# Group 3's high and low parts by converting and adding transfers, with the order of work laid out anew

## The chip, the core and the metric

The kernel runs on one core of a Trainium2 chip. The metric is the time of the whole program on the device in microseconds, the median of several executions. The engines are TensorE (PE, matrix products and transposes), VectorE (DVE), ScalarE (ACT) and GpSimd (POOL); SyncE (SP) only issues transfers. Each engine works off its own instructions in order and waits on semaphores for the others.

## The reference

Four steps on `x` of shape (4, 512, 256, 4) and a text `txt` of shape (4, 77, 256), all float32.

```python
h = einsum('bhid,oi,od->bho', x, weighted_sum, weight)      # tokens
h = concatenate([h, txt], axis=1)                            # 4 x 589 x 256
# attention-like block on n = layernorm(h)
hid  = relu(n @ gate_w1 + b1); gate = sigmoid(hid @ gate_w2 + b2)
glob = gate * (n @ U_w) * cumsum(n @ V_w, axis=1)
h = h + conv3(n, conv_w) + glob @ out_w + out_b
# quantised product on m = layernorm(h): int8 with a scale for each row of m
# and each column of rhs, exact integer product, then scaled back
h = h + int8_product(m, rhs)
```

## The kernel before

The 4 x 512 token rows are cut into eight **groups** of 256 (two to a batch, g0 to g7). A group's token product contracts over 1024 values: eight blocks of 128 (`kc` 0 to 7), each of which multiplies 2 x 128 rows by a 128 x 256 weight. Group 0 uses plain float32 products (L907). Groups 1 to 7 use three cheaper products for each block: `x_high` by `w_high` (L923), `x_high` by `w_low` (L925) and `x_low` by `w_high` (L927), where `x_high` is `x` rounded to a shorter format and `x_low` the rest. One block is called a **step** here: 64 steps in all, six products each from group 1 on. Blocks 0 to 3 of a group are its first half, 4 to 7 its second half; the halves are loaded and waited for apart.

There are two ways to the two parts. For groups 1 to 3, SyncE loads `x` into `x_sb` (L352), ScalarE rounds it into `x_high` (`chip_high`, L527), and VectorE (`chip_low`, L735) or, for group 3, GpSimd (`pool_low`, L435) subtracts. For groups 4 to 7 no engine sees `x`: GpSimd issues a transfer that converts `x` into `x_high` (`load_high`, L430), ScalarE writes minus `x_high` into `x_low` (`negate`, L538), and GpSimd issues a second transfer that adds `x` onto it (`add_x`, L441). Both parts lie in rings of three slots. The constant `BY_DMA` is the first group that goes the second way.

After its token product each group goes through statistics (VectorE, L709 and L712), one over the root of the variance and a shift (GpSimd, L404, L405, L463), normalising (ScalarE, L634), transposing (TensorE, L973), moving (ScalarE, L595), the hidden product (TensorE, L989), relu, running sums (VectorE, L784, L835), and for each batch the gate product (TensorE, L997), the sigmoid (ScalarE, L609) and the product of gate and sums (`gated`, GpSimd, L415, L421), which ScalarE and VectorE split in a high part (L618) and a low part (L818). Each batch then has three **items** (two of 256 rows, one of 77 text rows; 0 to 11): convolution (`local`, L1014) and output product (`mix`, L1027) on TensorE, a second layer norm, the row's maximum and step (VectorE, L824, L826, L828), rounding (GpSimd, L482), a transpose (L1041), conversion to integers (ScalarE, L627), the integer product (L1057), its scaling (VectorE, L861) and the last addition (`fin`, GpSimd, L495), then the store. For the last four items VectorE does the last addition itself (L851).

What is done in which order is written out by hand in the tables `GROUP_AT`, `ITEM_AT`, `TXT_AT`, `RHS_AT` and `WARM_AT`: a number for each stage and group or item, its **place**. Each engine runs through the places in rising order. On TensorE a step begins every 16 places, so that place 241 lies after step 15. On the others places are numbered more loosely. An instruction that has to wait holds up all behind it on its engine.

Of the kernel before, what the change touches and what calls it, by code (L numbers as in the profile page):

```python
# [10 lines left out]
ALU = mybir.AluOpType  # L11
# [23 lines left out]
    move=(7, 16, 27, 39, 51, 63, 75, 82),  # L35
    hidden=(321, 403, 497, 626, 754, 849, 1012, 1021),
    relu=(11, 20, 32, 42, 62, 66, 80, 84),
    sums=(11, 17, 27, 33, 46, 49, 62, 66),
    gates=(-1, 417, -1, 657, -1, 898, -1, 1023),
    sigmoid=(-1, 22, -1, 45, -1, 68, -1, 86),  # L40
    gated=(-1, 9, -1, 24, -1, 38, -1, 53),
    high=(24, 25, 49, 50, 69, 71, 89, 90),
    low=(19, 20, 37, 38, 54, 58, 69, 72),
    mid=(8, 18, 37, 40, 52, 67, 77, 83),
    tap0=(9, 15, 28, 31, 44, 50),
    tap2=(10, 16, 34, 36, 48, 51),
# [12 lines left out]
    put=(-1, -1, 33, -1, -1, 57, -1, -1, 79, -1, -1, 95),  # L59
    conv=(418, 467, 545, 722, 724, 817, 961, 1013, 1018, 1024, 1028, 1038),  # L60
    mix=(466, 468, 546, 723, 725, 818, 962, 1017, 1020, 1026, 1033, 1039),
    stats=(21, 22, 26, 39, 40, 47, 57, 64, 65, 71, 76, 79),
    rstd=(12, 16, 21, 30, 31, 40, 44, 50, 58, 59, 66, 67),
    centre=(28, 30, 36, 53, 55, 64, 73, 85, 87, 92, 98, 101),
    keep=(29, 31, 38, 54, 56, 65, 74, 93, 96, 97, 100, 104),
    scale=(24, 25, 29, 43, 45, 55, 61, 67, 70, 74, 78, 81),
    round=(15, 19, 22, 34, 37, 46, 47, 54, 57, 62, 65, 69),
    lscale=(17, 27, 28, 42, 43, 51, 52, 55, 60, 63, 68, 70),
    turn=(625, 659, 755, 897, 1011, 1015, 1019, 1027, 1031, 1037, 1042, 1045),
    ints=(43, 47, 58, 70, 76, 81, 88, 91, 94, 99, 102, 103),  # L70
    product=(658, 753, 820, 1010, 1014, 1022, 1025, 1029, 1035, 1040, 1043, 1046),
    out=(35, 42, 56, 60, 63, 68, 73, 75, 77, 80, 82, 83),
# [18 lines left out]
def early_fusion_kernel(nc, x0, x, ws, wt, txt, par, rhs, out, B, HI, T, D, ND, GH, R):  # L91
# [45 lines left out]
    with ExitStack() as ctx:  # L137
# [251 lines left out]
        def _(pool):  # L389
# [54 lines left out]
            for place in range(PLACES):  # L444
                for g in groups(place, "cast"):
                    load_high(g)
                for g in groups(place, "pool_low0"):
                    pool_low(g, 0)
                for g in groups(place, "pool_low1"):
                    pool_low(g, 1)  # L450
# [705 lines left out]
```

## Time and profile before

| | |
|---|---|
| median of 3 executions | 107.63 us (106.84 to 108.24) |
| profiled execution | 108.13 us, of which the span of the trace is 106.3 us |
| TensorE busy, of the span | 93.8 us, 88% |
| VectorE | 87.9 us, 83% |
| ScalarE | 76.2 us, 72% |
| GpSimd | 68.4 us, 64% |
| mean granted TensorE clock | 0.979 of 2.4 GHz |
| moved by the 16 DMA engines | 16.30 MB |

The busy time is what an engine's instructions took; what is not busy was waiting. Loads of weights on TensorE overlap its products. Time before the first and after the last traced instruction makes up the difference between 108.13 and 106.3.

### The profile page before, as it was taken

The numbers are of one execution on the slowest core, as the hardware profiler recorded it, in microseconds if no ns is written. First come the engines' busy times: TensorE is split into PE (matmuls) and PEld (weight loads), VectorE is DVE, ScalarE is ACT, GpSimd is POOL, SyncE is SP. The second block draws the span as 40 slices with busy tenths as digits, with TensorE's granted clock in tenths as the row PEclk, the third lists the DMA queues.
The fourth block names the chain that finished last, engine by engine and source line by source line (L and its number), as shares of the span: only waits on it lengthen the run. The fifth ranks groups of instructions, "written<-read, shape, count | busy, mean of one in ns | idle before, by whom it ended". The sixth has DMA issues, their size and how long they took to land.

```text
span 106.3 us, 2136 instructions
## 1 busy us (share of the span) xinstructions
PE 93.8 (88%) x686; PEld 85.4 (80%) x686; DVE 87.9 (83%) x224; ACT 76.2 (72%) x150; POOL 68.4 (64%) x131
## 2 busy tenths in 40 slices
PE   5999999998999999899945999699998889959780
PEld 5988899996969989899925999599896768849660
DVE  2456996969999887699999499999999999997731
ACT  1319739998979998899892969182898998656420
POOL 2000049099798469998993749903799979985840
PEclk9999999999999999999998599999999999999998
DMA  2999998038099499969959913894000050112223
GB/s 69 314 288 374 251 372 331 29 100 297 12 173 294 133 190 180 328 133 213 310 59 196 206 59 31 172 215 82 0 21 8 3 197 0 39 42 99 87 98 128
DMA packets 7849, 16.30 MB, mean 153 GB/s; under 512 B 823, under 2 KB 4767, under 8 KB 7839
## 3 DMA queue, kind: packets, MB, share of 16 engines
q0 software_dynamic: 2304, 8.39, 35.3%
q1 hardware_dynamic: 5103, 7.52, 21.3%
q10 hardware_dynamic: 432, 0.27, 0.9%
q8 instruction: 5, 0.08, 0.3%
q14 instruction: 5, 0.04, 0.1%
HBM read 13.76 MB, written 2.41 MB: 152 GB/s over the span
## 4 chain that ended last, share of the span: by engine, by line
PE 36%; DVE 20%; DMA 15%; POOL 10%; ACT 8%; issue 7%; SPq 0%; DVEq 0%; POOLq 0%
DMA x_sb<-x_dram 7%; DMA x_low<-x_dram 7%; PE h_ps L907 7%; DVE glob L818 4%; DVE convT L796 4%; PE acc_ps L1062 3%; DVE stats L709 3%; ACT xn L634 3%; POOL rstd L405 3%; PE h_ps L923 3%; POOL x_high L430 2%; PE h_ps L925 2%; PE h_ps L927 2%; DVE tmp L861 2%; PE uvg_ps L989 2%
## 5 line engine op out<-in xcount | busy, mean ns | idle before, releaser
L923 PE MATMUL h_ps<-w_high,x_high 128*128 128x256 f32 x112 | 33.7, 301 | 0.2 <-DMA x_low<-x_dram 0.2
L925 PE MATMUL h_ps<-w_low,x_high 128*128 128x256 f32 x112 | 31.8, 284 | 0.0
L927 PE MATMUL h_ps<-w_high,x_low 128*128 128x256 f32 x112 | 31.7, 283 | 0.0
L923 PEld LDWEIGHTS h_ps<-w_high,x_high 128*128 128x128 f32 x112 | 21.6, 193 | 1.0 <-issue 0.3
L925 PEld LDWEIGHTS h_ps<-w_low,x_high 128*128 128x128 f32 x112 | 21.7, 193 | 0.2
L927 PEld LDWEIGHTS h_ps<-w_high,x_low 128*128 128x128 f32 x112 | 21.6, 193 | 0.0
L405 POOL TENSOR_TENSOR rstd<-rstd,exponent 128x2 f32<-128x2 f32 (+2 forms) x21 | 16.3, 774 | 1.7
L404 POOL TENSOR_SCALAR rstd<-mv 128x2 f32<-128x2 f32 (+2 forms) x21 | 5.2, 249 | 17.9 <-DVE mv L712 17.0
L709 DVE BATCH_NORM_STATS2 stats<-h_ps 128x6 f32<-128x256 f32 (+1 forms) x36 | 13.7, 417 | 3.0 <-PE h_ps L927 2.1
L644 ACT ACTIVATE xc<-h_ps,mv 128x256 f32<-128x256 f32 (+1 forms) x20 | 8.6, 471 | 7.2 <-DVE mv L712 7.2
L796 DVE SCALAR_TENSOR_TENSOR convT<-xnT,par_sb,convT 128x255 f32<-128x255 f32 (+1 forms) x24 | 12.0, 548 | 0.8 <-ACT convT L588 0.7
L482 POOL TENSOR_SCALAR v<-xc,qmul 128x256 f32<-128x256 f32 (+1 forms) x20 | 10.9, 596 | 2.1 <-DVE qmul L828 1.8
L495 POOL TENSOR_TENSOR fin<-tmp,x_sb 128x512 f32<-128x512 f32 (+1 forms) x8 | 9.9, 1248 | 0.0
L634 ACT ACTIVATE xn<-h_ps,shift,rstd 128x256 f32<-128x256 f32 x16 | 8.1, 557 | 2.4 <-POOL shift L463 2.3
L441 POOL DMA_DIRECT2D x_low<-x_dram x8 | 7.6, 989 | 2.9 <-ACT x_low L538 2.7
L989 PE MATMUL uvg_ps<-xnT,par_sb 128*128 128x256 f32 x32 | 8.6, 391 | 1.0 <-issue 1.0
L588 ACT ACTIVATE convT<-xnT,par_sb 128x255 f32<-128x255 f32 (+1 forms) x16 | 9.3, 630 | 0.2
L538 ACT ACTIVATE x_low<-x_high 128x1024 fp32r<-128x1024 f32 x8 | 8.5, 1056 | 0.0
L618 ACT ACTIVATE glob<-glob 32x256 fp32r<-32x256 f32 (+1 forms) x16 | 7.2, 448 | 1.5 <-POOL glob L415 1.0
L1027 PE MATMUL h_ps<-outw,glob 96*128 96x256 f32 (+1 forms) x20 | 5.5, 344 | 2.7 <-DVE glob L818 2.7
L1014 PE MATMUL h_ps<-ident,convT 128*128 128x128 f32 (+1 forms) x40 | 7.9, 287 | 0.0
L907 PE MATMUL h_ps<-w_tok,x_sb 128*128 128x256 f32 x32 | 7.8, 405 | 0.0
(110 smaller groups left out, 217.2 us busy)
## 6 DMA issues: line engine op xcount, KB each, us to landing
x_high<-x_dram POOLq DMA_DIRECT2D x8, 512.0 KB, 5.2
x_low<-x_dram POOLq DMA_DIRECT2D x8, 512.0 KB, 5.6
x_sb<-x_dram SPq DMA_DIRECT2D x6, 512.0 KB, 7.5
out_dram<-fin SPq DMA_DIRECT2D x8, 256.0 KB
x_sb<-x_dram SPq DMA_DIRECT2D x3, 256.0 KB, 3.9
par_sb<-par_dram SPq DMA_DIRECT2D x1, 325.0 KB, 8.2
txt_sb<-txt_dram SPq DMA_DIRECT2D x1, 308.0 KB
out_dram<-fin SPq DMA_DIRECT2D x4, 77.0 KB
```

The lines of the kernel that those rows point to most:

```text
L405: nc.gpsimd.tensor_tensor(out_ap, out_ap, exponent[0:out_ap.shape[0], 0:out_ap.shape[1]], ALU.pow).then_inc(done, 1)
L482: last = nc.gpsimd.tensor_scalar(v[0:rows, j % 2, t, :], xc[0:rows, j % 4, t, :], qmul[0:rows, j, t:t + 1], ROUND + LOW_ZERO, ALU.mult, AL ...
L495: nc.gpsimd.tensor_tensor(fin[0:rows, j % 4, 0:nt, :], tmp[0:rows, j % 2, 0:nt, :], h2[0:rows, j % 4, 0:nt, :], ALU.add).then_inc(fin_pool, 1)
L588: nc.scalar.activation(convT[:, b % 2, c, lo:hi], xnT[:, c, b, 1 + lo:1 + hi], ACT.Identity, scale=conv[:, c, 1:2], bias=outb[:, c:c + 1]) ...
L634: last = nc.scalar.activation(xn[:, g % 2, t, :], h_of(g)[:, t, :], ACT.Identity, scale=rstd1[:, 2 * g + t:2 * g + t + 1], bias=shift1[:, ...
L709: last = nc.vector.bn_stats(stats[0:rows, t, :], src(t))
L796: nc.vector.scalar_tensor_tensor(out=convT[:, b % 2, c, lo:hi], in0=xnT[:, c, b, lo + tap:hi + tap], scalar=conv[:, c, tap:tap + 1], in1=c ...
L907: last = nc.tensor.matmul(h_of(g)[:, t, :], x_sb[:, g % X_SLOTS, kc, t * P:(t + 1) * P], w_tok[:, kc, :], start=(kc == 0 and t == 0), stop ...
L923: nc.tensor.matmul(h_of(g)[:, t, :], x_high[:, g % RING, kc, at], w_high[:, kc, :], start=(kc == 0 and t == 0), stop=False, skip_group_che ...
L925: nc.tensor.matmul(h_of(g)[:, t, :], x_high[:, g % RING, kc, at], w_low[:, kc, :], start=False, stop=False, skip_group_check=True)
L927: last = nc.tensor.matmul(h_of(g)[:, t, :], x_low[:, g % RING, kc, at], w_high[:, kc, :], start=False, stop=(kc == KC - 1), skip_group_che ...
L989: last = nc.tensor.matmul(uvg_ps[:, 0:PAIR], wcat[:, c, :], xnT[:, c, b, 1 + half * PAIR:1 + (half + 1) * PAIR], start=(c == 0), stop=(c = ...
```

## The change

Group 3 goes the second way: `BY_DMA` falls from 4 to 3. SyncE's two loads of group 3, ScalarE's two roundings and GpSimd's two subtractions go; two converting transfers, two negations on ScalarE and two adding transfers come. The function `pool_low` goes. All tables of places are new numbers, with the same stages in them.

```diff
 GROUP_AT = dict(
-    pool_low0=(-1, -1, -1, 4),
-    pool_low1=(-1, -1, -1, 6),
-    stats=(3, 6, 14, 23, 32, 41, 52, 59),
-    rstd=(0, 3, 8, 14, 23, 32, 39, 45),
-    norm=(5, 12, 23, 35, 48, 60, 72, 78),
-    turn=(241, 353, 465, 577, 721, 819, 1009, 1016),
+    stats=(2, 7, 14, 25, 32, 43, 53, 60),
+    rstd=(0, 4, 9, 16, 23, 32, 40, 47),
+    norm=(4, 13, 23, 36, 45, 60, 71, 79),
+    turn=(193, 322, 433, 593, 674, 817, 1009, 1017),
...
-    chip_high0=(-1, 1, 4, 10),
-    chip_high1=(-1, 2, 6, 15),
+    chip_high0=(-1, 1, 5),
+    chip_high1=(-1, 2, 7),
     chip_low0=(-1, 1, 5),
-    chip_low1=(-1, 2, 8),
-    cast=(-1, -1, -1, -1, 2, 7, 13, 20),
-    negate0=(-1, -1, -1, -1, 14, 26, 41, 59),
-    add0=(-1, -1, -1, -1, 5, 11, 25, 33),
-    negate1=(-1, -1, -1, -1, 21, 34, 44, 61),
-    add1=(-1, -1, -1, -1, 10, 18, 26, 36),
+    chip_low1=(-1, 3, 8),
+    cast=(-1, -1, -1, 1, 3, 8, 15, 22),
+    negate0=(-1, -1, -1, 10, 17, 29, 43, 59),
+    add0=(-1, -1, -1, 5, 7, 14, 27, 33),
+    negate1=(-1, -1, -1, 14, 22, 35, 49, 61),
+    add1=(-1, -1, -1, 6, 11, 17, 28, 35),
 )
...
-    fin=(29, 35, 41, 48, 49, 56, 61, 64),
+    fin=(30, 34, 41, 49, 51, 52, 63, 64),
...
-BY_DMA = 4
+BY_DMA = 3
...
             sp.dma_start(rhs_sb[:, :, :], rhs).then_inc(rhs_loaded, 16)
-            sp.wait_ge(tok_done, 1)
-            for n in range(2):
-                load_x(sp, 3, n)
...
-            def pool_low(g, n):
-                pool.wait_ge(chip_high_ready[n], g - PLAIN + 1)
-                nc.gpsimd.tensor_tensor(x_low[:, g % RING, HALF_KC[n], :], x_sb[:, g % X_SLOTS, HALF_KC[n], :],
-                                        x_high[:, g % RING, HALF_KC[n], :].bitcast(F32),
-                                        ALU.subtract).then_inc(chip_low_ready[g - PLAIN][n], 1)
```

**GpSimd's queue at the start**, from the root of group 0's variance on. L430 is the converting transfer, L441 the adding one, L435 the subtraction; before:

```order
L463 TENSOR_SCALAR shift<-mv,rstd 128x1 x2
L404 TENSOR_SCALAR rstd<-mv 77x4
L405 TENSOR_TENSOR rstd<-rstd,exponent 77x4
L430 DMA x_high<-x_dram 128x1024 x2
L404 TENSOR_SCALAR rstd<-mv 128x2
L405 TENSOR_TENSOR rstd<-rstd,exponent 128x2
L463 TENSOR_SCALAR shift<-mv,rstd 128x1 x2
L435 TENSOR_TENSOR x_low<-x_sb,x_high 128x1024
L441 DMA x_low<-x_dram 128x1024
L435 TENSOR_TENSOR x_low<-x_sb,x_high 128x1024
L430 DMA x_high<-x_dram 128x1024 x2
```

Now (L425 is the converting transfer, L430 the adding one):

```order
L448 TENSOR_SCALAR shift<-mv,rstd 128x1 x2
L425 DMA x_high<-x_dram 128x1024 x2
L399 TENSOR_SCALAR rstd<-mv 77x4
L400 TENSOR_TENSOR rstd<-rstd,exponent 77x4
L425 DMA x_high<-x_dram 128x1024 x2
L399 TENSOR_SCALAR rstd<-mv 128x2
L400 TENSOR_TENSOR rstd<-rstd,exponent 128x2
L448 TENSOR_SCALAR shift<-mv,rstd 128x1 x2
L430 DMA x_low<-x_dram 128x1024 x3
L425 DMA x_high<-x_dram 128x1024 x2
```

Group 3's two conversions stand ahead of the text's root, group 4's behind it, and both of group 3's additions and the first of group 4's in a row behind group 1's shift.

**GpSimd's queue in the middle**, from batch 1's product of gate and sums to item 0's last addition. Before:

```order
L415 TENSOR_TENSOR glob<-gate,us 64x256
L421 TENSOR_TENSOR glob<-gate_txt,us_txt 64x77
L441 DMA x_low<-x_dram 128x1024 x2
L474 TENSOR_TENSOR lscale<-nstep,rstd 128x2
L474 TENSOR_TENSOR lscale<-nstep,rstd 77x1
L495 TENSOR_TENSOR fin<-tmp,x_sb 128x512
```

Now:

```order
L410 TENSOR_TENSOR glob<-gate,us 64x256
L416 TENSOR_TENSOR glob<-gate_txt,us_txt 64x77
L467 TENSOR_SCALAR v<-xc,qmul 77x256
L399 TENSOR_SCALAR rstd<-mv 77x1
L400 TENSOR_TENSOR rstd<-rstd,exponent 77x1
L430 DMA x_low<-x_dram 128x1024 x2
L459 TENSOR_TENSOR lscale<-nstep,rstd 77x1
L480 TENSOR_TENSOR fin<-tmp,x_sb 128x512
```

Rounding of item 2 and its root now stand between the product and group 6's two adding transfers; the last addition of item 0 still follows these.

**ScalarE's queue at the same point**, from group 4's normalising on (L634, now L619). The high parts of batch 1 are L618 (now L603), a negation is L538 (now L523). Before:

```order
L634 ACTIVATE xn<-h_ps,shift,rstd 128x256 x2
L618 ACTIVATE glob<-glob 32x256 x2
L618 ACTIVATE glob<-glob 32x333 x2
L595 ACTIVATE xnT<-xt_ps 128x2x256
L588 ACTIVATE convT<-xnT,par_sb 128x255 x2
```

Now:

```order
L619 ACTIVATE xn<-h_ps,shift,rstd 128x256 x2
L603 ACTIVATE glob<-glob 32x256 x2
L612 ACTIVATE qT<-qt_ps 128x512
L603 ACTIVATE glob<-glob 32x333 x2
L523 ACTIVATE x_low<-x_high 128x1024
L580 ACTIVATE xnT<-xt_ps 128x2x256
```

The negation of group 6's second half, for which the second of the two adding transfers above waits, now stands behind the high parts of batch 1; before, both negations of group 6 were ahead of them.

## Rows read from the trace of the kernel before

**Rows 1.** The page, part 2: VectorE's busy tenths in 40 slices of the span.

```profile
DVE  2456996969999887699999499999999999997731
```

**Rows 2.** Timeline, TensorE: start, duration, line; in brackets its idle time and releaser.

```profile
25.46 0.66 PE L973 MATMUL xt_ps<-ident,xn 128*128 128x128 f32 x4 [0.43 <-ACT xn L634]
...
57.05 0.48 PE L1027 MATMUL h_ps<-outw,glob 96*128 96x256 f32 x2 [2.74 <-DVE glob L818]
...
68.81 1.10 PE L989 MATMUL uvg_ps<-xnT,par_sb 128*128 128x256 f32 x4 [0.96 <-issue]
```

**Rows 3.** The chain that ended last: start, duration, what.

```profile
29.51 0.63 PE uvg_ps L952 x2
...
30.95 1.00 PE uvg_ps L989 x4
...
53.64 3.28 DVE glob L818
...
58.76 0.21 PE h_ps L923
...
66.97 7.92 DMA x_low<-x_dram
...
78.66 0.12 PE h_ps L927
```

**Rows 4.** Timeline, GpSimd, beside that L818.

```profile
53.19 1.85 POOL L441 DMA_DIRECT2D x_low<-x_dram  x2
...
54.73 1.88 POOL L495 TENSOR_TENSOR fin<-tmp,x_sb 128x512 f32<-128x512 f32 x1
```

**Rows 5.** Timeline, VectorE and GpSimd, two other places.

```profile
34.96 0.92 POOL L441 DMA_DIRECT2D x_low<-x_dram  x1
...
35.43 0.41 DVE L818 TENSOR_TENSOR glob<-glob 32x256 fp32r<-32x256 f32 x1
...
65.42 1.91 DVE L826 TENSOR_SCALAR nstep<-amax 128x2 f32<-128x2 f32 x1
...
65.74 1.56 POOL L495 TENSOR_TENSOR fin<-tmp,x_sb 128x512 f32<-128x512 f32 x1
```

**Rows 6.** Stretches: length, busy time of each engine, TensorE's clock, DMA share, GB/s.

```profile
18.10:28.20 10.10, 9.67 (x77) 8.80 (x76) 8.68 (x19) 9.07 (x17) 6.66 (x10) 1.00 0.37 119
28.20:39.50 11.30, 11.30 (x83) 9.86 (x81) 10.51 (x31) 10.46 (x22) 8.45 (x14) 1.00 0.78 182
...
58.00:61.00 3.00, 3.00 (x16) 2.98 (x14) 1.59 (x8) 2.35 (x6) 1.89 (x4) 0.52 1.04 203
```

**Rows 7.** Timeline, group 0's product and its way to the normalising.

```profile
4.88 7.76 PE L907 MATMUL h_ps<-w_tok,x_sb 128*128 128x256 f32 x32
...
13.33 0.75 DVE L709 BATCH_NORM_STATS2 stats<-h_ps 128x6 f32<-128x256 f32 x2
...
15.67 0.51 POOL L463 TENSOR_SCALAR shift<-mv,rstd 128x1 f32<-128x1 f32 x2
...
16.43 1.01 ACT L634 ACTIVATE xn<-h_ps,shift,rstd 128x256 f32<-128x256 f32 x2
...
16.58 2.11 POOL L405 TENSOR_TENSOR rstd<-rstd,exponent 77x4 f32<-77x4 f32 x1
```

**Rows 8.** Groups by line: busy, mean ns of one.

```profile
L538 ACT ACTIVATE x_low<-x_high 128x1024 fp32r<-128x1024 f32 x8 | 8.5, 1056 | 0.0
...
L430 POOL DMA_DIRECT2D x_high<-x_dram x8 | 5.0, 658 | 2.6 <-DMA x_sb<-x_dram 2.6
L435 POOL TENSOR_TENSOR x_low<-x_sb,x_high 128x1024 fp32r<-128x1024 f32 x2 | 5.0, 2496 | 0.0
```

**Rows 9.** The page, part 3 (queue of GpSimd's transfers) and part 6 (issue to landing).

```profile
q0 software_dynamic: 2304, 8.39, 35.3%
...
x_high<-x_dram POOLq DMA_DIRECT2D x8, 512.0 KB, 5.2
x_low<-x_dram POOLq DMA_DIRECT2D x8, 512.0 KB, 5.6
```

More of the change, by code:

```diff
@@ L28 @@
 GROUP_AT = dict(
-    pool_low0=(-1, -1, -1, 4),
-    pool_low1=(-1, -1, -1, 6),
-    stats=(3, 6, 14, 23, 32, 41, 52, 59),
-    rstd=(0, 3, 8, 14, 23, 32, 39, 45),
-    norm=(5, 12, 23, 35, 48, 60, 72, 78),
-    turn=(241, 353, 465, 577, 721, 819, 1009, 1016),
[L35 to L46, printed above, removed]
-    chip_high0=(-1, 1, 4, 10),
-    chip_high1=(-1, 2, 6, 15),
-    chip_low0=(-1, 1, 5),
-    chip_low1=(-1, 2, 8),
-    cast=(-1, -1, -1, -1, 2, 7, 13, 20),
-    negate0=(-1, -1, -1, -1, 14, 26, 41, 59),
-    add0=(-1, -1, -1, -1, 5, 11, 25, 33),
@@ L54 @@
-    negate1=(-1, -1, -1, -1, 21, 34, 44, 61),
-    add1=(-1, -1, -1, -1, 10, 18, 26, 36),
+    stats=(2, 7, 14, 25, 32, 43, 53, 60),
+    rstd=(0, 4, 9, 16, 23, 32, 40, 47),
+    norm=(4, 13, 23, 36, 45, 60, 71, 79),
+    turn=(193, 322, 433, 593, 674, 817, 1009, 1017),
+    move=(6, 16, 26, 38, 50, 62, 76, 82),
+    hidden=(225, 369, 465, 625, 753, 849, 1012, 1021),
+    relu=(11, 20, 34, 41, 57, 65, 81, 84),
+    sums=(9, 16, 26, 34, 48, 52, 62, 67),
+    gates=(-1, 371, -1, 641, -1, 881, -1, 1023),
@@ new lines @@
+    sigmoid=(-1, 21, -1, 44, -1, 67, -1, 86),
+    gated=(-1, 10, -1, 24, -1, 39, -1, 54),
+    high=(24, 25, 46, 48, 69, 70, 89, 90),
+    low=(19, 20, 36, 38, 54, 57, 69, 72),
+    mid=(8, 19, 27, 40, 58, 63, 78, 83),
+    tap0=(10, 15, 23, 33, 45, 50),
+    tap2=(11, 18, 27, 35, 49, 51),
+    chip_high0=(-1, 1, 5),
+    chip_high1=(-1, 2, 7),
+    chip_low0=(-1, 1, 5),
+    chip_low1=(-1, 3, 8),
+    cast=(-1, -1, -1, 1, 3, 8, 15, 22),
+    negate0=(-1, -1, -1, 10, 17, 29, 43, 59),
+    add0=(-1, -1, -1, 5, 7, 14, 27, 33),
@@ L56 @@
+    negate1=(-1, -1, -1, 14, 22, 35, 49, 61),
+    add1=(-1, -1, -1, 6, 11, 17, 28, 35),
 )
 ITEM_AT = dict(
[L59 to L72, printed above, removed]
@@ L73 @@
-    fin=(29, 35, 41, 48, 49, 56, 61, 64),
-)
-TXT_AT = dict(turn=322, hidden=354, gates=401, stats=4, shift=7, uv=13, norm=9, move=13, relu=17,
-              sigmoid=19, rstd=1)
-RHS_AT = dict(turn=402, low=0, round=12, out=18, fold=30, fold_low=53, high=0, fold_high=46)
+    put=(-1, -1, 33, -1, -1, 56, -1, -1, 75, -1, -1, 93),
+    conv=(449, 451, 561, 689, 690, 755, 929, 1015, 1019, 1024, 1028, 1031),
+    mix=(450, 452, 577, 691, 694, 756, 930, 1016, 1020, 1025, 1029, 1034),
+    stats=(21, 22, 29, 39, 40, 46, 56, 64, 65, 71, 76, 79),
@@ new lines @@
+    rstd=(12, 13, 26, 36, 37, 38, 46, 56, 58, 60, 67, 68),
+    centre=(28, 31, 37, 51, 53, 64, 72, 85, 87, 94, 98, 101),
+    keep=(30, 32, 39, 52, 54, 66, 74, 91, 92, 96, 100, 102),
+    scale=(28, 30, 31, 41, 44, 58, 59, 68, 70, 74, 78, 81),
+    round=(18, 21, 25, 31, 44, 45, 50, 55, 61, 62, 66, 70),
+    lscale=(19, 20, 29, 42, 43, 48, 53, 57, 59, 65, 69, 71),
+    turn=(626, 673, 693, 754, 1010, 1014, 1022, 1026, 1032, 1037, 1041, 1045),
+    ints=(42, 47, 55, 73, 77, 80, 88, 95, 97, 99, 103, 104),
@@ L79 @@
+    product=(657, 692, 757, 1011, 1013, 1018, 1027, 1030, 1035, 1039, 1043, 1046),
+    out=(37, 42, 47, 61, 63, 66, 73, 75, 77, 80, 82, 83),
+    fin=(30, 34, 41, 49, 51, 52, 63, 64),
+)
+TXT_AT = dict(turn=289, hidden=321, gates=337, stats=4, shift=6, uv=13, norm=9, move=12, relu=15,
+              sigmoid=18, rstd=2)
+RHS_AT = dict(turn=370, low=0, round=12, out=17, fold=24, fold_low=55, high=0, fold_high=68)
 DIAG_AT = 3
-WARM_AT = {1030: 1, 1032: 1, 1034: 1, 1036: 2, 1041: 2, 1044: 2, 1047: 5, 1048: 7, 1049: 2, 1050: 1, 1051:
+WARM_AT = {1033: 1, 1036: 1, 1038: 1, 1040: 2, 1042: 2, 1044: 2, 1047: 5, 1048: 7, 1049: 2, 1050: 1, 1051:
@@ L285, in early_fusion_kernel @@
         chip_high_ready = [sem(f"chip_high_ready{n}") for n in range(2)]
-        chip_low_ready = [[sem(f"chip_low_ready{g}_{n}") for n in range(2)] for g in range(PLAIN, BY_DMA)]
+        chip_low_ready = [sem(f"chip_low_ready{n}") for n in range(2)]
         negated = [sem(f"negated{n}") for n in range(2)]
@@ L446, in _ @@
                     load_high(g)
[L447 to L450, printed above, removed]
                 for g in groups(place, "add0"):
@@ L913, in tok @@
                         pe.wait_ge(chip_high_ready[half_kc], g - PLAIN + 1)
-                        pe.wait_ge(chip_low_ready[g - PLAIN][half_kc], 1)
+                        pe.wait_ge(chip_low_ready[half_kc], g - PLAIN + 1)
                     elif kc % (KC // 2) == 0:
```

2 lines of the change are left out of this document (1 added, 1 removed).

## The prediction

> **What bounds the kernel now.** I read the page first: TensorE is busy 88% of the span and VectorE 83%, so neither alone explains 106.3 us. The slices say when: from the middle of the span on, VectorE is at 9 nearly throughout [rows 1], while before that TensorE is the engine without gaps. So up to the last token products the time is TensorE's work plus its holes, and behind it a tail that VectorE paces. Second, the idle times in TensorE's timeline: the largest before that tail is 2.74 us before L1027 at 57.05, and the reader is to see its releaser, VectorE's L818; the others shown are 0.43 and 0.96 us [rows 2]. Third, the chain that ended last, which passes through the same place: one L818 of 3.28 us at 53.64, where its like takes 0.41 [rows 3, 5]. Fourth, the stretches: behind that hole TensorE's clock is granted at 0.52 (its lower level, 1.2 GHz) from 58 to 61, and a product comes every 0.21 us instead of 0.12 [rows 3, 6]. Without that one late L818 the hole would be gone and most likely the slow stretch.
>
> **Why L818 is late.** GpSimd issues two adding transfers from 53.19 on and then runs item 0's last addition, 54.73 to 56.61; L818 ends at 56.92, just behind it [rows 3, 4]. The same picture stands at 65.42: L826, a tensor_scalar on two values per row, takes 1.91 us and ends at 67.33, just behind another last addition that ends at 67.30 [rows 5]. Issuing a transfer does no such thing by itself: at 35.43 an L818 takes 0.41 us inside an L441 of 34.96 to 35.88 [rows 5]. So I put the delay down to GpSimd's long elementwise instructions. What this doesn't explain is that L818 had begun 1.1 us before the addition did, when only transfers were being issued; that doubt is a rival below. The Trainium skill (GPSIMD Engine Reference, Specifications) says that GpSimd shares its SBUF interfaces with VectorE and contends with VectorE instructions in a 2-port mode or with two SBUF inputs. By that rule a VectorE instruction with two SBUF inputs beside any long GpSimd elementwise instruction is at risk, the removed subtractions included; the rows agree for L818 but show no general stall, and by the rule alone I could name no place in the new order that is safe.
>
> **Part 1, the engines' work.** GpSimd loses two subtractions, 2 x 2.50 = 5.0 us, and gains two conversions (2 x 0.66) and two additions (2 x about 0.92): 3.2 us, so 1.8 us less [rows 5, 8]. It is not the bound there; I cost it at nothing, and its cover is GpSimd's own idle time. ScalarE trades two roundings for two negations of 1.06 us; I take a rounding at the same price, so nothing [rows 8]. VectorE's instructions stay the same. SyncE's two loads of group 3 have nothing late behind them, since the stores come much later: nothing.
>
> **Part 2, the transfers.** GpSimd's queue took 35.3% of the span for 16 transfers of 512 KB, 0.353 x 106.3 / 16 = 2.35 us of all 16 DMA engines each [rows 9]. Four more cost 9.4 us of DMA time, less what the two plain loads took. There is room for about two and a half of them from 18.1 to 28.2 (share 0.37, so 6.4 us free) and for one from 28.2 to 39.5 (share 0.78, 2.5 us free) [rows 6]. So they fit, barely. In time: group 3's conversions go out behind group 0's shift, which ended at 16.18 and now about 0.65 earlier, so at about 15.5 and 16.2, and land 5.2 later, by 21.4. The negation (1.06), the issue (0.92) and the addition's landing (5.6) make 7.6 more [rows 5, 7 to 9]. The second half also waits on ScalarE's queue behind group 1's normalising, whose transpose began at 25.46 before [rows 2]; its addition goes out at about 26.2 and lands at 31.8, or at 34.1 with the 7.9 us of the last addition in the trace [rows 3]. TensorE needs the first half at about 32 and the second at about 34.5: group 3 began near 28.2, and the small products for text, rhs and hidden values that then stood inside it (29.51 to 31.95, four pieces, 2.4 us) plus the gates' now come ahead of it [rows 3]. So 2.7 us in hand for the second half, or 0.4 at worst. Cost nothing, with up to 0.5 in the range. In this case the Trainium skill (DMA: Bandwidth & Descriptors, Issuing engines are not separate DMA queues) speaks against the change: transfers from all issuers run on the same 16 DMA engines. The shares above say the same of this kernel, and it stays a cost only where the margin is used up.
>
> **Part 3, group 0's transpose is put three steps earlier** (place 241 to 193). TensorE gets there after five steps of group 1: from about 12.4 on, where group 0's products drain, 30 products at 0.12, so at 15.9 to 16.0. Its input is ScalarE's normalising. VectorE's statistics of group 0 ran at 13.33, behind the last `chip_low`; now they stand ahead of it and can start when group 0's product ends, 4.88 + 7.76 = 12.64 [rows 7]. The normalising started 3.10 after the statistics and lasted 1.01, so it ends at 12.7 + 3.1 + 1.0 = 16.8 to 16.9 [rows 7]. TensorE waits about 1.0 us: **+1.0**. Bounds: 0 if it were ready, 1.5 if it came as late as before (17.44).
>
> **Part 4, the middle.** The hole of 2.74 goes, and 3.8 us of work at half clock (57.05 to 60.9) become 1.9: **-2.7 and -1.9** [rows 2, 3, 6]. The reason is the order. Item 0's last addition still follows group 6's two adding transfers, but the second of these now waits for a negation which ScalarE does only after the high parts of batch 1. VectorE's L818s need only these high parts, so they are done before GpSimd can reach the addition. Bounds: -4.6 to 0. What is late next on TensorE is its own work, since the low part now comes about when the transposes of both items of convolution end.
>
> **Part 5, small ones.** The wait of 0.43 before group 1's transpose goes, as the text's products now stand between it and group 0's: **-0.4**. That of 0.96 before group 5's hidden product came behind the stretched L826 and goes if no last addition falls on item 4's step; half: **-0.5** (0 to -1.0) [rows 2, 5]. Group 7's additions: the last landed after 7.92 us, 0.1 us before TensorE could use it [rows 3]. When TensorE is 4 us earlier, they must be earlier too; GpSimd issues them behind group 5's shift, which moves with the products, but the DMA engines carry more. **+0.7** (0 to 1.5). VectorE follows with what L818 and the idle time behind it had cost, so the tail keeps its length. Last, the trace has other VectorE instructions stretched like these two, by up to 1.7 us, and the new order deals them anew: I add **+0.7** for one of about 1.5 us that falls on the path in half the cases, an estimate from these rows [rows 3, 5].
>
> **The sum.** +1.0 - 2.7 - 1.9 - 0.4 - 0.5 + 0.7 + 0.7 = -3.1. On the profiled execution's 108.13 us that gives 105.0 us, its span about 103.2. That execution was 0.5 us above the median of the three, 107.63, against which 105.0 is 2.4% less. With the bounds of the parts this case reaches from 102.8 to 106.5.
>
> **Rivals.**
> - **The hole goes, but its gain is used up elsewhere** (chance 0.34). A last addition falls on another VectorE instruction that TensorE waits for (+1.7 as at 65.42), group 7's second half comes 1.5 late rather than 0.7, and the 0.96 stays. Then 105.0 + 1.7 + 0.8 + 0.5 = 108.0; with only some of it 106 to 108. For it: GpSimd still runs eight last additions. Against it: in the trace of before only one of the stretched instructions made TensorE wait long.
> - **The change doesn't take the late L818 away** (0.08). If issuing transfers while the rings are full stops VectorE, what counts is L441 next to L818, and that pair is still near. Then the 4.6 stay: 109.6. Against it is the L818 of 0.41 us beside an L441 [rows 5].
> - **Group 3 comes late, slower** (0.10). Place: TensorE's steps 24 and 28. The path through GpSimd's queue has two waits in a row for negations, with group 4's addition, group 5's conversions and group 2's root behind. It decides when the second half lands after 34.5, by two landings of about 7.9 instead of 5.2 and 5.6: 2.7 + 2.3 = 5.0 against 2.7 in hand, a hole of 2.3 us, after which the clock can fall as it did behind 2.74 (+1.9). Group 4 and 5 then take the same queue late, once more 2.3. 105.0 + 2.3 + 1.9 + 2.3 = 111.5; half of it gives 108.3. The DMA share of 0.78 behind 28.2 speaks for it, the 0.37 before it against.
>
> **How the numbers follow.** The forecast has 0.48, the rivals 0.34, 0.08 and 0.10. About 2% (2.15 us) is what a measurement of this kernel can tell from no change: faster means under 105.5, slower over 109.8. Of the forecast about three quarters lie under 105.5, and a little of the first rival: 0.40. Slower: most of the last rival and a part of the second: 0.09. The rest, 0.51, is within 2%. The predicted time is the forecast's, 105.0. The range of eight in ten runs from 103.0 to 108.4: it leaves out the forecast's lowest end and the two dear rivals.
>
> **What would show it.** TensorE's timeline should show about 1.0 us of idle time before the first transpose of `xn`; no wait over 0.5 us before steps 24 and 28; all eight L818s (now L803) at 0.4 to 1.0 us; TensorE's clock at 1.00 from 50 to 65; the last token product 3 to 4 us before 78.66 [rows 3]; the same length of tail behind it. The forecast is wrong if an L818 stays long, if a wait for `x_low` of group 3 or 7 goes over 2 us, or if the tail, counted from the last token product, grows by over 1 us.

## The result, and the profile after

| | before | after |
|---|---|---|
| median | 107.42 us (106.84 to 108.24, 4 executions) | 104.34 us (103.68 to 105.32, 4 executions) |
| profiled execution, span | 108.13, 106.3 us | 104.53, 102.7 us |
| TensorE, VectorE busy | 93.8, 87.9 us | 92.3, 82.5 us |
| ScalarE, GpSimd busy | 76.2, 68.4 us | 76.1, 70.1 us |
| mean granted clock | 0.979 | 0.996 |

The ratio is 0.969, 95% interval 0.962 to 0.977: 3.1% faster. Medians, here and below, are over all executions of a kernel, while ratios and their intervals leave out the slow executions on both sides. The forecast was 105.0 us (103.0 to 108.4). Run again beside the variations below, the changed kernel took 104.57 us against 107.66, ratio 0.967 (0.958 to 0.976).

The page after, part 2: the busy tenths of VectorE (before in [rows 1]) and the clock.

```profile
DVE  3377694489979988996999999899978988998731
PEclk9999999999999999999999999999999999999998
```

VectorE's nearly unbroken 9s from slice 21 on are gone. It lost 5.4 us of busy time with the same 224 instructions, so that was time held, not work. The largest parts, by the durations of single instructions, which overlap a little, are 3.0 us at L818, 1.8 at L826 and 1.6 at an instruction beside one of group 3's subtractions in the trace of before. It is a tensor_scalar on two values per row, which takes 0.17 us after, and it ended just behind the subtraction (26.70 against 26.68); nothing on TensorE waited for it:

```profile
24.98 1.72 DVE L744 TENSOR_SCALAR rscale<-rmax 128x2 f32<-128x2 f32 x1
```

```profile
24.31 2.37 POOL L435 TENSOR_TENSOR x_low<-x_sb,x_high 128x1024 fp32r<-128x1024 f32 x1
```

The clock has no dip before the last slice.

The waits of TensorE after, from its timeline (start, duration, line; idle time and its releaser in brackets), for [rows 2]:

```profile
17.42 0.66 PE L958 MATMUL xt_ps<-ident,xn 128*128 128x128 f32 x4 [1.29 <-ACT xn L619]
...
46.49 0.66 PE L958 MATMUL xt_ps<-ident,xn 128*128 128x128 f32 x4 [0.86 <-ACT xn L619]
...
75.83 0.28 PE L912 MATMUL h_ps<-w_high,x_low 128*128 128x256 f32 x1
```

The 2.74 before the output product (L1012 now) and the 0.96 before group 5's hidden product are gone; 1.29 before group 0's transpose is new. Waits not shown, up to the last token product, are 0.67 us before a gate product at 32.04, 0.27 at 53.20 and 0.39 at 60.57. The last row is the last token product, which stood at 78.50 before.

VectorE and GpSimd after, at the place where [rows 4] show the held L818 (L803 now; L430 is the adding transfer, L480 the last addition):

```profile
53.75 0.58 DVE L803 TENSOR_TENSOR glob<-glob 32x256 fp32r<-32x256 f32 x1
54.37 0.88 DVE L846 SCALAR_TENSOR_TENSOR tmp<-acc_ps,lscale,rs_row 128x256 f32<-128x256 f32 x2
55.28 0.49 DVE L803 TENSOR_TENSOR glob<-glob 32x333 fp32r<-32x333 f32 x1
```

```profile
55.03 0.95 POOL L430 DMA_DIRECT2D x_low<-x_dram  x1
56.91 0.88 POOL L430 DMA_DIRECT2D x_low<-x_dram  x1 [0.93 <-ACT x_low L523]
57.47 0.53 POOL L459 TENSOR_TENSOR lscale<-nstep,rstd 77x1 f32<-77x1 f32 x1
57.62 1.62 POOL L480 TENSOR_TENSOR fin<-tmp,x_sb 128x512 f32<-128x512 f32 x1
```

Both low parts are over (55.77) when GpSimd gets to the last addition (57.62). Of the 1.85 us between, 0.93 is its wait for ScalarE's negation, as the prediction said; the rest comes from the rounding and root of item 2, which also stand ahead of it now. All eight L803 lie between 0.41 and 0.59 us.

The stretches after, with the columns of [rows 6]:

```profile
18.10:28.20 10.10, 10.02 (x77) 8.77 (x76) 8.21 (x19) 9.79 (x19) 7.71 (x11) 1.00 0.82 227
28.20:39.50 11.30, 10.63 (x82) 10.08 (x82) 10.03 (x30) 10.26 (x21) 6.55 (x12) 1.00 1.04 239
50.00:65.00 15.00, 14.32 (x121) 13.23 (x120) 14.30 (x38) 13.70 (x27) 12.33 (x22) 1.00 0.80 189
58.00:61.00 3.00, 2.61 (x23) 2.15 (x21) 2.90 (x8) 2.69 (x8) 2.18 (x3) 1.00 1.04 198
```

The DMA share went from 0.37 to 0.82 and from 0.78 to 1.04 in the first two, yet TensorE's waits before L908, the first product that needs new parts, are 0.1 us in all. From 58 to 61 the clock is 1.00 (2.4 GHz), where it was 0.52.

The page after, parts 3 and 6, for [rows 9]:

```profile
q0 software_dynamic: 2880, 10.49, 43.5%
...
x_high<-x_dram POOLq DMA_DIRECT2D x10, 512.0 KB, 6.4
x_low<-x_dram POOLq DMA_DIRECT2D x10, 512.0 KB, 6.1
```

There are twenty transfers now, 0.435 x 102.7 / 20 = 2.23 us of all 16 engines each, and by the medians they land 0.5 to 1.2 us later than before.

### The profile page after: what moved, and what is told of

The parts are those of the page before. It is cut to its first block, busy times and chain, and to the rows that moved or that the text cites. A ratio compares the mean times of both kernels' runs of the same rounds, so it can differ in the third digit from the quotient of the medians.

```text
span 102.7 us, 2135 instructions
## 1 busy us (share of the span) xinstructions
PE 92.3 (90%) x686; PEld 83.8 (82%) x686; DVE 82.5 (80%) x224; ACT 76.1 (74%) x150; POOL 70.1 (68%) x133
## 4 chain that ended last, share of the span: by engine, by line
ACT 23%; POOL 19%; PE 16%; DVE 13%; DMA 11%; issue 10%; SPq 4%; POOLq 0%; ACTq 0%
DMA x_sb<-x_dram 11%; POOL rstd L400 7%; ACT xn L619 4%; ACT x_low L523 4%; POOL rstd L399 4%; POOL x_high L425 4%; SPq L350 3%; DVE stats L694 3%; PE h_ps L1003 3%; ACT convT L573 2%; POOL shift L448 2%; ACT xc L629 2%; DVE amax L809 2%; ACT tmp L531 2%; ACT glob L603 2%
## 5 line engine op out<-in xcount | busy, mean ns | idle before, releaser
L908 PE MATMUL h_ps<-w_high,x_high 128*128 128x256 f32 x112 | 33.8, 302 | 0.1
L910 PE MATMUL h_ps<-w_low,x_high 128*128 128x256 f32 x112 | 31.3, 279 | 0.0
L908 PEld LDWEIGHTS h_ps<-w_high,x_high 128*128 128x128 f32 x112 | 21.1, 188 | 1.0 <-issue 0.8
L910 PEld LDWEIGHTS h_ps<-w_low,x_high 128*128 128x128 f32 x112 | 21.1, 189 | 0.2
L912 PEld LDWEIGHTS h_ps<-w_high,x_low 128*128 128x128 f32 x112 | 21.1, 188 | 0.0
L399 POOL TENSOR_SCALAR rstd<-mv 128x2 f32<-128x2 f32 (+2 forms) x21 | 8.6, 410 | 17.4 <-DVE mv L697 16.7
L619 ACT ACTIVATE xn<-h_ps,shift,rstd 128x256 f32<-128x256 f32 x16 | 8.1, 559 | 6.3 <-POOL shift L448 6.3
L430 POOL DMA_DIRECT2D x_low<-x_dram x10 | 9.1, 910 | 3.4 <-ACT x_low L523 3.3
L467 POOL TENSOR_SCALAR v<-xc,qmul 128x256 f32<-128x256 f32 (+1 forms) x20 | 10.1, 531 | 0.8 <-DVE qmul L813 0.5
L523 ACT ACTIVATE x_low<-x_high 128x1024 fp32r<-128x1024 f32 x10 | 10.5, 1052 | 0.0
L480 POOL TENSOR_TENSOR fin<-tmp,x_sb 128x512 f32<-128x512 f32 (+1 forms) x8 | 9.9, 1250 | 0.0
L603 ACT ACTIVATE glob<-glob 32x256 fp32r<-32x256 f32 (+1 forms) x16 | 7.2, 447 | 1.0 <-POOL glob L410 0.6
L809 DVE TENSOR_REDUCE amax<-xc 128x2 f32<-128x512 f32 (+1 forms) x12 | 7.0, 586 | 0.9 <-ACT xc L629 0.8
L958 PE MATMUL xt_ps<-ident,xn 128*128 128x128 f32 x32 | 5.1, 281 | 2.9 <-ACT xn L619 2.9
```

The lines of the kernel that those rows point to most:

```text
L399: then_wait(nc.gpsimd.tensor_scalar(out_ap, var_ap, LN_EPS, None, ALU.add))
L467: last = nc.gpsimd.tensor_scalar(v[0:rows, j % 2, t, :], xc[0:rows, j % 4, t, :], qmul[0:rows, j, t:t + 1], ROUND + LOW_ZERO, ALU.mult, AL ...
L523: nc.scalar.activation(x_low[:, g % RING, HALF_KC[n], :], x_high[:, g % RING, HALF_KC[n], :], ACT.Copy, scale=-1.0).then_inc(negated[n], 1)
L619: last = nc.scalar.activation(xn[:, g % 2, t, :], h_of(g)[:, t, :], ACT.Identity, scale=rstd1[:, 2 * g + t:2 * g + t + 1], bias=shift1[:, ...
L908: nc.tensor.matmul(h_of(g)[:, t, :], x_high[:, g % RING, kc, at], w_high[:, kc, :], start=(kc == 0 and t == 0), stop=False, skip_group_che ...
L910: nc.tensor.matmul(h_of(g)[:, t, :], x_high[:, g % RING, kc, at], w_low[:, kc, :], start=False, stop=False, skip_group_check=True)
```

## The experiments

**Theories.** A: the gain comes from one fact of the order, that item 0's long last addition on GpSimd no longer stands beside batch 1's low part on VectorE. B: the low part was held by the issue of the adding transfers. C: the gain comes from taking group 3's subtractions off GpSimd. Each ratio is to the kernel before on the same chip; a line of the changed kernel has a number 2 to 15 lower than before, because `pool_low` and a load are gone.

### The last addition alone

```diff
-    fin=(29, 35, 41, 48, 49, 56, 61, 64),
+    fin=(31, 35, 41, 48, 49, 56, 61, 64),
```

The kernel before, with item 0's last addition two places later.

> The kernel before with one number changed: item 0's last addition on GpSimd stands behind the roots of items 3 and 4 instead of ahead of them. These roots need batch 1's low parts, so the addition can't run beside the L818s of batch 1. The two adding transfers of group 6 stay right beside them. Theory A (the long last addition on GpSimd holds L818): all L818s at 0.4 to 1.0 us, no hole of 2.74 us on TensorE, clock 1.00 from 58 to 61, and 3.0 to 4.6 us less than before. Rival B (issuing the adding transfers holds L818): L818 still about 3.3 us, hole and slow clock stay, time within 1 us of before. Rival C (the gain came from taking group 3's subtractions off GpSimd): no gain here either.

Measured: 104.44 us (103.62 to 105.08), ratio 0.974 (0.965 to 0.984), span 103.1. VectorE's and GpSimd's timelines at the place:

```profile
52.94 0.45 DVE L818 TENSOR_TENSOR glob<-glob 32x256 fp32r<-32x256 f32 x1
53.57 0.49 DVE L818 TENSOR_TENSOR glob<-glob 32x333 fp32r<-32x333 f32 x1 [0.18 <-ACT glob L618]
```

```profile
52.50 1.86 POOL L441 DMA_DIRECT2D x_low<-x_dram  x2
53.74 0.98 POOL L474 TENSOR_TENSOR lscale<-nstep,rstd 128x2 f32<-128x2 f32 x2
...
57.21 1.27 POOL L495 TENSOR_TENSOR fin<-tmp,x_sb 128x512 f32<-128x512 f32 x1
```

The two adding transfers stand beside the low part and the `lscale` pair right behind them, as before, and the low part takes 0.45 us; only the addition has gone. All eight L818 are at 0.41 to 0.50 us. A holds. B is out, and so is C as the source of the gain: one number gives 2.6%, with group 3 still done the old way. The whole change gives 3.1%, and the two intervals overlap, so it is not shown that the rest of it adds anything. The clock keeps 1.00 from 50 to 65.

The gain is at the lower end of what theory A expected (3.0 to 4.6 us), because TensorE now waits for the transfers' landing: 0.60 us for `x_low` of group 6, 0.38 for group 7's first half and 1.58 for its second. Counted without the wait there, TensorE comes 4.9 us earlier to group 6 than before (58.10 - 0.60 for 62.40), and as much to group 7; GpSimd issues the additions only 0.7 us earlier for group 6 and 3.1 for group 7.

### The last addition in two halves

```diff
-                        nc.gpsimd.tensor_tensor(fin[0:rows, j % 4, 0:nt, :], tmp[0:rows, j % 2, 0:nt, :],
-                                                h2[0:rows, j % 4, 0:nt, :], ALU.add).then_inc(fin_pool, 1)
+                        for t in (range(nt) if j == 0 else [slice(0, nt)]):
+                            last = nc.gpsimd.tensor_tensor(fin[0:rows, j % 4, t, :], tmp[0:rows, j % 2, t, :],
+                                                           h2[0:rows, j % 4, t, :], ALU.add)
+                        last.then_inc(fin_pool, 1)
```

> The kernel before, with item 0's last addition on GpSimd as two instructions of 128x256 values instead of one of 128x512; nothing moves, and the same values are added. It asks how long VectorE's low part (L818) is held. If a held instruction of VectorE waits for the end of one GpSimd instruction, the long L818 ends behind the first half: about 1.0 to 1.3 us shorter than 3.3 us, the hole before the output product shrinks from 2.7 to about 1.5 us, and the time falls by 1 to 3 us (the slow clock may go too): 104.5 to 106.5 us. If VectorE is held until GpSimd has no elementwise work any more, or is merely slowed in proportion to the overlap, L818 stays at 3.0 to 3.5 us, the hole at 2.5 us and more, and the time at 107.6 within 0.5.

Measured: 105.85 us (105.71 to 107.59), ratio 0.984 (0.972 to 0.996), span 104.0, no slow clock in the profiled execution. VectorE, GpSimd and TensorE at the place (L820 is the low part, L496 the halves):

```profile
53.38 2.10 DVE L820 TENSOR_TENSOR glob<-glob 32x256 fp32r<-32x256 f32 x1
...
55.50 0.92 DVE L820 TENSOR_TENSOR glob<-glob 32x333 fp32r<-32x333 f32 x1
```

```profile
54.47 2.52 POOL L496 TENSOR_TENSOR fin<-tmp,x_sb 128x256 f32<-128x256 f32 x2
```

```profile
55.62 0.47 PE L1029 MATMUL h_ps<-outw,glob 96*128 96x256 f32 x2 [1.56 <-DVE glob L820]
```

The first low part is let go 1.2 us earlier (2.10 for 3.28), the hole shrinks from 2.74 to 1.56, and the next low part is held a little by the second half (0.92 for 0.49). So VectorE is let go when one GpSimd instruction ends, and not when GpSimd has no more work. The hole and the clock (1.7, see below) should give 1.2 + 1.7 = 2.9 us; the span fell by 2.3, because the wait before group 5's hidden product, behind another last addition, grew from 0.96 to 1.38 and others appeared. The clock's share is not isolated by this: two other executions of this kernel, at 105.93 and 105.71 us, had mean clocks of 0.980 and 0.983, where the profiled one had 1.000, and were as fast.

### The last addition earlier, in the changed kernel

```diff
-    fin=(30, 34, 41, 49, 51, 52, 63, 64),
+    fin=(26, 34, 41, 49, 51, 52, 63, 64),
```

> The changed kernel with one number changed: item 0's last addition stands directly ahead of group 6's two adding transfers, about where batch 1's second low part runs. Theory A: the second L803 of batch 1 is stretched by the addition to 1.5 us or more, and TensorE waits for it before the output product of item 4; the adding transfers of group 6 go out 1.3 us later. 1 to 3 us slower than the changed kernel, and the clock may fall if the hole reaches 2.7. Rivals B and C: no stretched L803; within 1 us of the changed kernel.

Measured: 107.91 us, the median of ten executions. Two took 104.93 and 105.39, the other eight 107.0 to 108.84; the ratio, 0.981 (0.973 to 0.989), is that of the two. The trace is of one of the eight (107.0 us, span 105.2). In it the low parts are not held, against my expectation: the addition could only start when its input was there.

```profile
53.89 0.49 DVE L803 TENSOR_TENSOR glob<-glob 32x333 fp32r<-32x333 f32 x1
```

```profile
53.94 1.60 POOL L480 TENSOR_TENSOR fin<-tmp,x_sb 128x512 f32<-128x512 f32 x1 [0.25 <-DVE tmp L846]
55.49 1.85 POOL L430 DMA_DIRECT2D x_low<-x_dram  x2
```

```profile
62.58 0.35 PE L908 MATMUL h_ps<-w_high,x_high 128*128 128x256 f32 x1 [2.96 <-DMA x_low<-x_dram]
```

Here VectorE's instruction began first, and it was the addition that took 1.60 us, where four of the kernel's other additions of this size take 1.26 or 1.27. But the addition stood ahead of group 6's adding transfers. The first of them went out 1.6 us behind the second low part (53.89 to 55.49), in the changed kernel 0.25 us ahead of it (55.03 to 55.28). They landed after 7.0 and 8.8 us, there after 5.6 and 6.2. TensorE waited 2.96 us, and its clock was granted at 0.62 from 62 to 66. So this run tells nothing on A. Nor does it settle the price of the place: by the two lower executions the kernel is only 0.6 to 1.1 us above the changed one's median, and their interval touches its (0.962 to 0.977); whether they had the wait of 2.96 us isn't known, as no trace was taken of them. What the trace of the changed kernel does show is how little it has in hand: the first of group 6's adding transfers lands at 60.6 (55.03 + 5.6) and TensorE's step 48 begins at 61.30. For group 7 it is 0.1 us in each half (68.7 against 68.80, 72.9 against 73.05).

### The new order with the old way, and the reverse

```diff
 # new order, old way: the changed kernel with pool_low and its loads back
-BY_DMA = 3
+BY_DMA = 4
+    pool_low0=(-1, -1, -1, 5),
+    pool_low1=(-1, -1, -1, 6),
+    chip_high0=(-1, 1, 5, 10),
+    chip_high1=(-1, 2, 7, 14),
...
 # old order, new way: the kernel before without pool_low and its loads
-BY_DMA = 4
+BY_DMA = 3
+    cast=(-1, -1, -1, 1, 2, 7, 13, 20),
+    negate0=(-1, -1, -1, 10, 14, 26, 41, 59),
+    add0=(-1, -1, -1, 4, 5, 11, 25, 33),
+    negate1=(-1, -1, -1, 15, 21, 34, 44, 61),
+    add1=(-1, -1, -1, 6, 10, 18, 26, 36),
...
```

> The new order of work with group 3's parts made the old way: SyncE's loads, ScalarE's roundings where the negations stood, GpSimd's subtractions where the adding transfers stood. Theory A: the hole is gone here too, so most of the gain stays: 104 to 105.5 us. The two subtractions of 2.5 us in a row on GpSimd delay the root of group 2 by about 3 us and may cost up to 1.5 us. Rival C: without the new way there is no gain: 107 us or more.

> The old order with group 3's parts made the new way: conversions, negations and adding transfers at the places of the old loads, roundings and subtractions. Theory A: the late L818 beside item 0's last addition stays, with its hole and slow clock: 106 to 109 us, no gain over 1.5 us. Rival C: the gain comes with the new way alone: 104 to 105.5 us.

| | old order | new order |
|---|---|---|
| subtractions for group 3 | 107.57 | 110.09 (ratio 1.021, 1.012 to 1.030) |
| transfers for group 3 | 110.55 (ratio 1.033, 1.024 to 1.042) | 104.34 |

(107.57 is the kernel before beside these runs; 104.34 the changed kernel against 107.42.)

New order, old way: the low parts are normal (0.41 to 0.59), as A says, but I had expected 104 to 105.5 and the kernel is slower than before. VectorE, GpSimd and TensorE, where the two subtractions (L435) now stand in a row:

```profile
24.66 5.93 DVE L796 SCALAR_TENSOR_TENSOR convT<-xnT,par_sb,convT 128x255 f32<-128x255 f32 x4
```

```profile
25.16 5.15 POOL L435 TENSOR_TENSOR x_low<-x_sb,x_high 128x1024 fp32r<-128x1024 f32 x2
```

```profile
34.19 2.04 PE L989 MATMUL uvg_ps<-xnT,par_sb 128*128 128x256 f32 x4 [4.24 <-DVE sum_txt L761]
```

Four convolution taps of VectorE, which read `xnT` and `convT` from SBUF and take some 0.5 us each otherwise, take 5.93 together: two of them are normal, and two last 2.61 and 2.60 us, about the length of one subtraction (2.50) each. All behind them, the text's sums last, is late, TensorE waits 4.24 us, and from 34 to 37 its clock is granted at 0.50. It is the mechanism of the held L818 at a second place, and it takes back more than the hole had cost.

Old order, new way: the hole stays, and group 3 comes late.

```profile
29.38 0.35 PE L908 MATMUL h_ps<-w_high,x_high 128*128 128x256 f32 x1 [2.06 <-DMA x_low<-x_dram]
...
36.47 0.35 PE L908 MATMUL h_ps<-w_high,x_high 128*128 128x256 f32 x1 [0.61 <-DMA x_low<-x_dram]
...
58.97 0.48 PE L1012 MATMUL h_ps<-outw,glob 96*128 96x256 f32 x2 [2.72 <-DVE glob L803]
```

The longest L803 is 3.26 us beside `L480`. This is what A forecasts for the hole. The time, 110.55, is above the 106 to 109 us that I expected, because TensorE also waits for group 3. That shows the place and the size of my rival "group 3 comes late": without the order that puts the text's and gates' products ahead of it, its parts arrive 2.06 us after TensorE. So neither half of the change gains alone. Each brings a loss that the other removes, while the single move of the first experiment gains without either.

### Two waits of the changed kernel

The changed kernel with group 0's transpose and hidden product two steps later (`turn[0]` 193 to 225, `hidden[0]` 225 to 257); with the root of group 3 earlier on GpSimd (`rstd[3]` 16 to 14); with both; and unchanged.

> The changed kernel, with group 0's transpose two steps later (place 225 instead of 193) and its hidden product too (257 instead of 225). It measures what the three steps earlier cost. By the theory that TensorE's wait of 1.29 us before that transpose is on the path: 12 more products of group 1 of 0.12 us (1.44 us) now cover it, the wait is 0 to 0.1 us, and the time falls by 0.8 to 1.3 us against the changed kernel, since TensorE has no large hole of its own up to the middle. By the rival, that this order has slack elsewhere which a lead is only given back to (the later hidden product and running sums hold back what follows them, or group 2 and 3 then wait for their parts): the wait is gone too, but the time falls by less than 0.3 us, and new waits stand before x_low of group 2 or 3 or before the text's transposes.

> The changed kernel, with the root of group 3's variance two places earlier on GpSimd (14 instead of 16), ahead of the conversions of group 6. It is for TensorE's wait of 0.86 us before group 3's transpose at 46.5 us, which the forecast did not have. If GpSimd's queue is what makes group 3's normalising late, that wait shrinks to under 0.3 us and the time falls by 0.3 to 0.6 us; the price is that group 6's conversions go out up to 1 us later. If ScalarE's own queue makes it late, nothing changes: 0.8 to 0.9 us of wait, and the same time within 0.3 us.

> Both of these moves in the changed kernel: group 0's transpose and hidden product two steps later, and the root of group 3 two places earlier. If both waits are on the path and nothing is given back: 1.1 to 1.9 us less than the changed kernel, about 102.4 to 103.2 us, the fastest of all. If the transfers' margin is what then ends the wait (TensorE arrives earlier at groups 6 and 7, whose adding transfers are issued by a queue that does not get faster): 0 to 0.5 us less, with waits for x_low of 0.5 us and more from group 5 on.

> The changed kernel once more, on the same chip as its two variations (group 0's transpose later, group 3's root earlier), so that differences of a few tenths are read against a neighbour and not against another chip's run. All theories: 104.3 us within 0.7, ratio to the kernel before 0.965 to 0.975; the waits of 1.29, 0.67 and 0.86 us on TensorE within 0.1 of what they were.

| | median us | ratio to before |
|---|---|---|
| unchanged | 104.57 | 0.967 (0.958 to 0.976) |
| transpose later | 104.00 | 0.965 (0.958 to 0.972) |
| root earlier | 104.02 | 0.970 (0.963 to 0.977) |
| both | 103.45 | 0.962 (0.955 to 0.968) |

The first wait goes, but 0.94 us come back three microseconds later, for the low part of group 2's first half (L720); with only the transpose later:

```profile
20.32 0.36 PE L908 MATMUL h_ps<-w_high,x_high 128*128 128x256 f32 x1 [0.94 <-DVE x_low L720]
```

That is the new wait its rival expected. The gain of 0.6 us in the medians is under the 0.8 to 1.3 of the theory, above the rival's 0.3, and inside the interval, so it decides nothing. The root earlier:

```profile
52.37 0.66 PE L958 MATMUL xt_ps<-ident,xn 128*128 128x128 f32 x4 [0.92 <-ACT xn L619]
```

Group 3's wait (0.86) is gone and group 4's grew from 0.27 to 0.92, here and in the run with both moves. The unchanged kernel in this comparison had no wait before group 3's transpose either, and 1.08 us before group 0's, so against my expectation these waits differ between executions by 0.2 to 0.9 us, and 0.86 was no fixed property of the order. With both moves the median, 103.45, is above the 102.4 to 103.2 that I expected if nothing were given back; it is 4.2 us under before and the lowest of all, but its interval overlaps that of the changed kernel: no gain over it is shown.

## Why the prediction was right, step by step

It was right: 104.34 against 105.0, by the mechanism that carried it. The profiled span fell by 3.6 us: the last token product starts 78.50 - 75.83 = 2.7 us earlier, where 3 to 4 was named as the sign, and the tail behind it is 0.9 us shorter, where the same length was. These are one profiled execution of each kernel. The changed kernel profiled again had a span of 101.1 us for 102.7, so a few tenths in a term mean little. By its terms:

| term | forecast | trace after |
|---|---|---|
| 1 engines' work | 0 | VectorE 5.4 us less; GpSimd 1.7 more, where 1.8 less was forecast; no wait from it shown beyond term 3 |
| 2 transfers | 0 | 0; no wait for group 3 |
| 3 group 0's transpose | +1.0 | +1.3 |
| 4 hole and slow clock | -2.7, -1.9 | -2.7, -1.7 |
| 5 wait of 0.43; wait of 0.96 | -0.4; -0.5 | -0.4; -1.0 |
| 5 group 7's additions | +0.7 | 0 (0.17 us before, 0.1 after) |
| 5 a new collision | +0.7 | +1.9: 0.67, 0.27 and 0.39 new, and 0.86 for 0.33; other waits than meant |
| tail | 0 | -0.9 |

The terms as measured give -2.6 up to the last token product, against -2.7.

That the total came so near is partly luck. The collision term was 1.2 us too small and its waits are of another kind: the forecast meant a held VectorE instruction that TensorE waits for, and these waits are for ScalarE and GpSimd. The 0.7 for group 7's additions was not needed, and the tail paid back 0.9 that nobody had forecast. The wait of 0.43 went as forecast, but not shown to be for the reason given: it is also missing in the traces of the first experiment, of the split addition and of the old order with the new way, which all keep the order at that place.

**Part 4 is shown for the hole**, not only argued: moving the addition alone takes it away, the old order keeps it, and halving the addition shortens it by 1.2 us. The clock's part is only worked out. The forecast took 57.05 to 60.9 as work at half clock; the windows have 0.97 from 57.0 to 57.5, 0.50 up to 60.5 and 0.62 from 60.5 to 61.0, so 3.4 us at half clock, worth 1.7 and not 1.9. And two executions of the kernel before with a mean clock of 1.000 took 106.81 and 106.83 us, only 0.9 below the medians beside them (107.66 and 107.72).

The doubt named there, that L818 began 1.1 us before the addition, stays open. In the run with two halves the low part again began 1.1 us before the recorded start of L496, and ended at 55.48, 0.3 us behind the start recorded for the second half (55.2). The profile calls GpSimd's spans rough, and L474 and L495 overlap in them. The hold is also longer than what it is put down to: 3.28 less 0.41 is 2.9 us, and the addition is recorded with 1.88 and takes 1.25 elsewhere. The Trainium skill (SBUF — State Buffer, Who interferes with whom) says that a VectorE instruction with two SBUF inputs contends with a GpSimd instruction that reads SBUF, that the pair of SBUF ports which the two share goes to whoever issues first for its whole instruction, and that the other fully blocks. The taps agree with a whole instruction (2.61 beside a subtraction of 2.50), and both directions occur (1.60 for the addition above, 1.02 for L399 below). By the recorded starts VectorE was first at L818 and blocked all the same, and whether the rule or the recorded start is off no run here shows. The Trainium skill (Perfetto Trace Analysis, GPSIMD Engine Instruction) warns that a GpSimd instruction's span in the profile is unreliable.

**Part 3 was 0.3 short.** I had VectorE's statistics followed by the normalising in 3.1 us; it took 3.7 (12.67 to 16.35). GpSimd's work on group 0's variance now stands beside VectorE's subtraction for group 1's second half:

```profile
13.64 1.19 DVE L720 TENSOR_TENSOR x_low<-x_sb,x_high 128x1024 fp32r<-128x1024 f32 x1
```

```profile
13.89 1.02 POOL L399 TENSOR_SCALAR rstd<-mv 128x2 f32<-128x2 f32 x1 [12.36 <-DVE mv L697]
```

The tensor_scalar on two values per row, 0.23 us elsewhere, took 1.02 and ended 0.08 behind VectorE's subtraction. It looks like the same hold the other way round, which no experiment here tested by itself, and I had looked for it in one direction only.

**Part 1's GpSimd** went up by 1.7 us, not down by 1.8, for this reason: its small instructions were held in places (1.02, 1.10 and 0.81 for 0.23), and the first instruction of the roots took 8.6 us in all where it had taken 5.2. Beyond part 3 no wait of TensorE is shown to come from it, though the root ahead of the wait of 0.86 has such an instruction too (0.80 at 43.07).

**Part 2** was right in its result: group 3 is in time. Its path has an error. Group 0's shift ended at 16.3 for 15.5, and GpSimd then waited 0.83 us for the loads into `x_sb`, a wait that the forecast didn't have, so the conversions went out from 17.15 on. The adding transfers and the step that needs the second one:

```profile
24.95 0.94 POOL L430 DMA_DIRECT2D x_low<-x_dram  x1
27.31 0.87 POOL L430 DMA_DIRECT2D x_low<-x_dram  x1 [1.42 <-ACT x_low L523]
```

```profile
35.73 0.36 PE L908 MATMUL h_ps<-w_high,x_high 128*128 128x256 f32 x1
```

The second landed 6.0 us after its issue, at 33.3 for 31.8. TensorE was later too, at 35.73 for 34.5, so 2.4 us were in hand where 2.7 were forecast. The Trainium skill's rule that all issuers share the 16 DMA engines (DMA: Bandwidth & Descriptors, Issuing engines are not separate DMA queues) fits the shares of 1.04 and the later landings, but the margin held. The old order with the new way shows what happens without it: 2.06 us late.

**The tail** was my miss of 0.9 us in the other direction. I let VectorE's pace decide and looked for no move of items there. Between the last token product and the end TensorE's waits before were 3.8 us and are 2.5 now; the one of 1.28 us (of "issue", before an L1062 at 95.59) is gone, as it is in every trace of the new order, while each of the old order has it (1.27 to 1.29). From the transpose of group 7's `xn` to the end of the span it is 22.5 us after and 22.6 in the new order with the old way, but 23.4 before, 23.4 in the old order with the new way, and 23.5 with the last addition moved alone. So it is the order's, and which move in it made it was not tried.

**The rivals.** "The gain is used up elsewhere" took place on a small scale (1.9 us in the collision term for 0.7), and the tail paid it back. "The change doesn't take the late L818 away" is out by the first experiment. "Group 3 comes late" is a true mechanism, which the order in the change avoids.

## What to carry to other kernels

When a tiny VectorE instruction takes several times its like, look at what GpSimd runs beside it, and the other way round; then move the long one behind the short one that others wait for, since one place in a table did here what the rewrite of a group's input path did not do alone. After such a gain look at the transfers that did not get earlier by as much: here TensorE waited up to 1.58 us for the adding ones. And test each half of a combined change, since the "way" lost 3% and the "order" 2% apart, and they gained 3% together.

## What the runs showed of the hardware

- Instructions of VectorE and GpSimd that run side by side can hold each other. A low part of 0.41 us took 3.28 beside GpSimd's addition and 2.10 beside the halved one, a tap of about 0.5 took 2.61 beside a subtraction, a tensor_scalar on two values per row of 0.17 took 1.91 and 1.72, and on GpSimd the first instruction of a root, 0.23, took 1.02. The issue of two adding transfers beside a low part did nothing (0.45 us).
- In the profiled executions TensorE's clock fell to half behind holes of 2.74, 2.72, 2.96 and 4.24 us (mean 0.50 to 0.62 over the next three or four), and not behind those of 1.56 and 2.06 us.
- With 20 transfers of 512 KB on GpSimd's queue instead of 16 (DMA share 0.82 and 1.04 in two stretches that had 0.37 and 0.78), the converting ones landed after 6.4 us (median) instead of 5.2, the adding ones after 6.1 instead of 5.6.
